# RNN and LSTM in one kernel: from step 48 on, the RNN's input products of 8 steps as seven block products

## The chip, the core and the metric

The kernel runs on one core of a Trainium2 chip. The metric is the device time of one execution in microseconds; smaller is better. Five engines work from queues of their own, each in order: TensorE (PE, with its weight loads as PEld), VectorE (DVE), ScalarE (ACT), GpSimd (POOL), and SyncE (SP), which issues transfers here.

## What is computed

A tanh RNN over 128 steps of x (32 x 128 x 512), its output added to x, then an LSTM over the sum, its output added again. All matrices have 512 rows.

```python
def step(prev_h, xw):                      # RNN, xW = x @ Wx + b
    next_h = jnp.tanh(prev_h @ Wh + xw)
...
x = x + rnn(x, cond_1024, ...)
...
a = xw_t + prev_h @ Wh                     # LSTM, xW = x @ Wx + b, four gates
next_c = f * prev_c + i * g
next_h = o * jnp.tanh(next_c)
...
x = x + lstm(x, cond_1024, ...)
```

## The kernel before

**Steps.** One loop over k runs both networks: iteration k does RNN step k and LSTM step k - LAG, with LAG = 7. x comes in groups of TG = 4 steps (one tile xb, 128 partitions x 512: four slices of 32 batch rows). Every engine has its own copy of the loop, so that the order in each queue is the order in which the functions are called there. "Even" and "odd" below are of k. For k from 27 on the pattern repeats every two steps, apart from work that comes once in a group of 4 steps or rarer.

**Precision.** float32 factors are split into a high and a low float16 half; a product is high x high + high x low (of the weights) + low x high. Each half is scaled by powers of two: the peaks of x over groups of steps are found by `peak_of_x` on VectorE, sent by SyncE through a row on one partition (`peaks_to_row`, `reduce_row`, `peaks_to_all`) and turned into scales (`x_power`, `x_products`, `x_inverses`). Before, one such exchange serves 4 groups (`BATCHES`).

**TensorE in one step.** With 32 batch rows, a matmul has a stationary of 128 x 32 and writes 32 partitions (`quarter(j)`); four of them stand side by side in the array, which is column-tiled. In the order of the queue in step k:
- `recurrent_l(k - 7)`: 48 matmuls with 512 columns, the last 16 with hT_lo;
- for the LSTM's input, pairs of steps are computed by seven block products in place of eight (`block_product`): in an even step 36 matmuls with 256 columns stand here (the rest of block 2, and block 3), in an odd one 60 (the first part of block 2, and blocks 6 and 4);
- `product_r16(k + 1)`: the RNN's input product of the next step, 24 matmuls with 256 columns into the RNN's bank, from x16, the halves of the turned x;
- `recurrent_r16(k)`: 24 matmuls with 256 columns on the RNN's state; the first 16 use hT_r_hi and the last 8 hT_r_lo, for which it waits on `rnn_lo`;
- block 7 in an odd step, blocks 1 and 5 in an even one.

The RNN's outputs come in two halves on other partitions, which `other_half_out` (ScalarE) and `rnn_add_r16` (VectorE) put together.

**ScalarE in one step.** The gates of LSTM step k - 7, a seed or copy for the pairs, tanh of c, once in 4 steps `x16_hi` (k = 4g - 2), in odd steps `y_pair_hi`, xr in two parts, tanh of the RNN, copies and seeds for the pairs, `seed_r(k + 2)` (bias and zeros into the RNN's bank), `rnn_h_hi(k)` (hT_r_hi). Then the next step's gates.

**VectorE in one step.** fc, ig and c of the cell, `rnn_h_lo(k - 1)` (hT_r_lo), h_hi and hT_hi, h_l, h_lo and hT_lo, pre_r, sums for the pairs, once in four steps each `turn_x` (k = 4g - 4), a peak (k = 4g - 19) and `x16_lo` (k = 4g - 2), `y_pair_lo`, the turned hT_r, the scale work.

**GpSimd** adds both outputs to xb and makes the blocks for the pairs. **SyncE** stores group g when it is done, then loads group g + 8 in its place.

## Time and profile before

| | us |
|---|---|
| median of 3 runs | 846.83 |
| lowest, highest | 844.51, 846.87 |
| profiled execution | 844.77 |
| its span in the profile | 843.0 |
| TensorE busy | 827.6 (98%) |
| VectorE busy | 602.5 (71%) |
| ScalarE busy | 578.9 (69%) |
| GpSimd busy | 289.0 (34%) |

A busy TensorE is not one at its peak: matmuls are pipelined and their ends modelled. In an order of time, a line stands for several instructions of one form; the next line's start says more of the pace than the length does. An idle time in brackets names who ended it. Idle time of an engine that nobody waits for costs nothing.

### The profile page before, as it was taken

How to read it: one execution, taken by the hardware profiler on the slowest of the kernel's cores; microseconds unless marked ns; L12 is line 12 of the kernel's file. 1: busy time of each engine (PE TensorE's matmuls, PEld its weight loads, DVE VectorE, ACT ScalarE, POOL GpSimd, SP SyncE). 2: the span in 40 equal slices, each digit the busy share in tenths (PEclk: the TensorE clock that was granted, in tenths of full speed). 3: DMA queues.
4: the chain of work that ended last, by engine and by line, in shares of the span. 5: the costliest groups of instructions: out<-in, count | busy, mean ns of one | idle time of the engine just before them, and what ended most of it. 6: DMA issues, size and time to landing. Idle time of an engine off the chain costs nothing.

```text
span 843.0 us, 52000 instructions
## 1 busy us (share of the span) xinstructions
PE 827.6 (98%) x22859; PEld 620.9 (74%) x22859; DVE 602.5 (71%) x1722; ACT 578.9 (69%) x1542; POOL 289.0 (34%) x642
## 2 busy tenths in 40 slices
...
DMA packets 40195, 30.70 MB, mean 36 GB/s; under 512 B 5772, under 2 KB 38688, under 8 KB 38688
## 3 DMA queue, kind: packets, MB, share of 16 engines
...
q14 instruction: 48, 0.39, 0.2%
q10 hardware_dynamic: 256, 0.11, 0.0%
...
## 4 chain that ended last, share of the span: by engine, by line
PE 90%; DMA 4%; DVE 3%; ACT 2%; issue 1%; SPq 0%; ACTq 0%; DVEq 0%
PE ps_l L1290 34%; PE ps_l L1356 29%; PE ps_r L1442 9%; PE ps_r L1462 8%; PE ps_l L1334 3%; PE ps_l L1303 2%; PE ps_l L1323 2%; DMA wxl_raw<-in_L_cond_Wx 2%; DMA whl_raw<-in_L_cond_Wh 2%; DMA whr_raw<-in_L_cond_Wh 1%; PE ps_r L1413 1%; PE ps_r L1424 1%; DVE ig L1092 0%; PE ps_l L1277 0%; DVE fc L1090 0%
## 5 line engine op out<-in xcount | busy, mean ns | idle before, releaser
L496 POOL TENSOR_TENSOR xb<-xb,h_l 128x128 f32<-128x128 f32 x127 | 58.2, 458 | 383.8 <-DVE h_lo L1125 379.4
L1090 DVE TENSOR_TENSOR fc<-gates,c 128x128 f32<-128x128 f32 x128 | 39.6, 309 | 150.4 <-ACT gates L780 136.5
L1356 PE MATMUL ps_l<-whl_raw,wxl_raw 128*32 128x256 f16 x3816 | 131.6, 273 | 0.0
L1290 PE MATMUL ps_l<-whl_hi,hT_hi 128*32 128x512 f16 x1888 | 122.5, 379 | 1.1 <-DVE hT_hi L1109 1.1
L1290 PE MATMUL ps_l<-whl_hi,hT_lo 128*32 128x512 f16 x1888 | 122.5, 379 | 0.0
L1290 PE MATMUL ps_l<-whl_lo,hT_hi 128*32 128x512 f16 x1888 | 122.4, 379 | 0.0
L1356 PE MATMUL ps_l<-wxl_hi,wxl_raw 128*32 128x256 f16 x2544 | 115.8, 273 | 0.0
L1356 PEld LDWEIGHTS ps_l<-whl_raw,wxl_raw 128*32 128x32 f16 x3816 | 102.1, 97 | 2.2 <-issue 0.2
L780 ACT ACTIVATE gates<-ps_l,g_products 128x256 f32<-128x256 f32 x114 | 53.5, 469 | 54.2 <-PE ps_l L1290 54.1
L1290 PEld LDWEIGHTS ps_l<-whl_lo,hT_hi 128*32 128x32 f16 x1888 | 51.1, 97 | 50.8
L1290 PEld LDWEIGHTS ps_l<-whl_hi,hT_lo 128*32 128x32 f16 x1888 | 51.1, 97 | 50.8
L557 POOL TENSOR_TENSOR whr_raw<-xT,hT_r 128x128 f32<-128x128 f32 x108 | 50.3, 465 | 110.7 <-DVE hT_r L1151 110.7
L532 POOL TENSOR_TENSOR whr_raw<-whr_raw 128x64 f32<-128x64 f32 x216 | 81.2, 396 | 4.2
L1356 PEld LDWEIGHTS ps_l<-wxl_hi,wxl_raw 128*32 128x32 f16 x2544 | 68.4, 97 | 17.6 <-issue 0.2
L803 ACT ACTIVATE h_r<-pre_r 128x128 f32<-128x128 f32 x114 | 35.3, 310 | 65.0 <-DVE pre_r L1136 65.0
L738 ACT ACTIVATE xr<-ps_r,g_products 64x128 f32<-64x128 f32 x114 | 41.5, 364 | 49.1 <-PE ps_r L1442 48.2
L1356 PE MATMUL ps_l<-wxl_lo,wxl_raw 128*32 128x256 f16 x1272 | 71.8, 273 | 0.0
L1290 PEld LDWEIGHTS ps_l<-whl_hi,hT_hi 128*32 128x32 f16 x1888 | 50.7, 97 | 27.3 <-DVE hT_hi L1109 1.3
L1151 DVE STREAM_TRANSPOSE hT_r<-h_r 128x128 f32<-128x128 f32 x128 | 52.6, 411 | 16.7 <-ACT h_r L803 16.6
L762 ACT ACTIVATE hT_r_hi<-hT_r,g_inverses 128x128 f16<-128x128 f32 x114 | 45.5, 399 | 27.7 <-DVE hT_r L1151 23.6
L505 POOL TENSOR_TENSOR xb<-xb,h_r 128x128 f32<-128x128 f32 x128 | 61.7, 482 | 0.0
L1105 DVE SCALAR_TENSOR_TENSOR h_hi<-gates,g_inverses,tanh_c 128x128 f16<-128x128 f32 x122 | 42.9, 352 | 21.7 <-ACT tanh_c L795 15.0
...
## 6 DMA issues: line engine op xcount, KB each, us to landing
xb<-in_x SPq DMA_DIRECT2D x128, 64.0 KB, 2.2
out<-xb SPq DMA_DIRECT2D x124, 64.0 KB, 1.8
...
wxl_raw<-peaks SPq DMA_DIRECT2D x5, 2.0 KB, 2.6
```

The costliest lines, as they stand in the source:

```text
L496: nc.gpsimd.tensor_tensor(xb[g % NX][:, t, :], xb[g % NX][:, t, :], h_l[s % 2][:, :], ALU.add).then_inc(out_done, 1)
L505: nc.gpsimd.tensor_tensor(xb[g % NX][:, t, :], xb[g % NX][:, t, :], h_r[r % 2][:, :], ALU.add).then_inc(y_done, 1)
L532: nc.gpsimd.tensor_tensor(y[:, out, :, :], y[:, a, :, :], y[:, b, :, :], op).then_inc(y_blocks, 1)
L557: nc.gpsimd.tensor_tensor(yA[g % 2][:, first:first + 2, :, t // 2, :], xT[g % 2][:, :, t, :].rearrange("p (a k) b -> p a k b", a=2), hT_r[ ...
L762: nc.scalar.activation(hT_r_hi[:, :, :], hT_r[:, :, :], ACT.Copy, scale=g_scale_r[:, OF_H, g:g + 1]).then_inc(rnn_hi, 1)
L780: nc.scalar.activation(gates[:, 0:2 * P], sums[:, 0:2 * P], ACT.Sigmoid, scale=unscale_l(s)).then_inc(lstm_act, 1)
L1105: nc.vector.scalar_tensor_tensor(out=h_hi[:, :], in0=gates[:, 2 * P:3 * P], scalar=factor, in1=tanh_c[:, :], op0=ALU.mult, op1=ALU.mult).t ...
L1151: nc.vector.transpose(hT_r[:, :, :], by_chunk(h_r[r % 2][:, :])).then_inc(rnn_hT, 1)
L1290: last = nc.tensor.matmul(ps_l[s % 4][quarter(j), :], (hT_hi, hT_lo)[h_part][:, k, :], gate_slice(whl[w_part][k], j), start=False, stop=(h ...
L1356: last = nc.tensor.matmul(at[quarter(j), :], stationary, weights[:, j, :, :], start=False, stop=(y_part == 1 and k == 1), skip_group_check ...
L1442: last = nc.tensor.matmul(ps_r[r % 2][quarter(2 * p + c), 0:2 * P], (hT_r_hi, hT_r_lo)[h_part][:, 2 * p + k, :], quadrant_of_r16(wr[OF_H][ ...
L1462: last = nc.tensor.matmul(ps_r[r % 2][quarter(2 * p + c), 0:2 * P], x16[x_part][g % 2][:, 2 * p + k, t * B:(t + 1) * B], quadrant_of_r16(w ...
```

## The change

From step 48 on, 8 steps (an octet, q = 6 to 15, steps 8q to 8q + 7) have their RNN input products computed as 2 x 2 blocks: the rows are two groups of 4 steps (128 rows each), the inputs and the outputs are halves of 256. Seven block products replace eight (the scheme that the LSTM pairs use already), one in each of the steps 8q - 9 to 8q - 3. All other work of an octet stands ahead of them or behind, by a distance in steps (`ahead(k, ticks)` gives q where k = 8q - ticks):

- 13 and 12: `turn_block` (VectorE) turns the groups 2q and 2q + 1 into a ring of five tiles; 12 and 11: `x_sum` (GpSimd), four sums of 128 x 256.
- 10: `x_rows_high`, `seed_xa` (ScalarE), `x_rows_low` (VectorE). 9: `copy_xm1`, `x_sums_high` part 0, `seed_xd`, `x_sums_low` part 0. 8: `take_xm5`, `x_sums_high` part 1, `x_sums_low` part 1. 7: `copy_xu2`. 6 and 5: `add_xm5`, `add_xu3` (VectorE).
- 4 and 3: `take_x` (ScalarE) copies a bank of 128 x 512 to SBUF; SyncE's `x_inputs` rearranges it by 16 transfers of 32 x 128 into `xin`; `seed_xin` (ScalarE) puts this into the RNN's bank in place of bias and zeros.

Each `x_block` on TensorE is 6 matmuls with a stationary of 128 x 128 and 256 columns, ahead of `recurrent_r16`. The banks ps_pk and ps_end serve for them; a fill opens ps_pk. `product_r16` ends with step 47, `x16_hi` and `x16_lo` with group 11, `turn_x` too. In steps 27 to 33, sums and differences of the RNN's weights are made and split. The peak exchange serves 2 groups from group 12 on, and stands 8 steps earlier.

```diff
-        BATCHES = [(G1, 3)] + [(g, 4) for g in range(4, NG, 4)]
+        BATCHES = [(G1, 3), (4, 4), (8, 4)] + [(g, 2) for g in range(GX, NG, 2)]
...
-        TURN_X_AT.update({4 * g - 4: g for g in range(3, NG)})
+        TURN_X_AT.update({4 * g - 4: g for g in range(3, GX)})
...
-        X16_AT.update({4 * g - 2: g for g in range(RG + 1, NG)})
+        X16_AT.update({4 * g - 2: g for g in range(RG + 1, GX)})
+
+        XW_AT = {27: (0, 1), 28: (2,), 29: (3, 4), 30: (5,), 31: (6, 7)}
+        XW_HALVES_AT = {32: (0, 1), 33: (2, 3)}
+        BIAS_X_AT = 30
+        X_ORDER = (1, 5, 6, 2, 7, 3, 4)
...
+            def x_inputs(q, half):
+
+                sp.wait_ge(x_out, 2 * (q - XQ) + half + 1)
+                sp.wait_ge(xin_zeroed, 1)
+                if q > XQ:
+                    sp.wait_ge(r_seeded, seeds_of_r(8 * (q - 1) + 4 * half + 3))
+                for t in range(TG):
+                    for j in range(J):
+                        sp.dma_start(xin[quarter(j), 4 * half + t, 0, :],
+                                     x_wide[half][quarter(t), j * P:(j + 1) * P]).then_inc(xin_loaded[half], DMA)
...
+                if g % 2 == 0 and XQ <= g // 2 + 1 < NG // 2:
+                    x_inputs(g // 2 + 1, 1)
+                if g % 2 == 1 and XQ <= (g + 3) // 2 < NG // 2:
+                    x_inputs((g + 3) // 2, 0)
...
+            def seed_xin(r):
+                act.wait_ge(rnn_pre, r - 1 - R0)
+                act.wait_ge(xin_loaded[r % 8 // TG], DMA * J * TG * (r // 8 - XQ + 1))
+                nc.scalar.activation(ps_r[r % 2][:, 0:2 * P], xin[:, r % 8, :, :].rearrange("p z u -> p (z u)"),
+                                     ACT.Copy).then_inc(r_seeded, 1)
...
-                if RS <= k + 2 < T:
+                if RS <= k + 2 < 8 * XQ:
                     seed_r(k + 2)
+                if 8 * XQ <= k + 2 < T:
+                    seed_xin(k + 2)
                 if R0 - 1 <= k < T - 1:
                     rnn_h_hi(k)
+                for i in XW_HALVES_AT.get(k, []):
+                    wxr_high(i)
+                if ahead(k, 10) is not None:
+                    x_rows_high(ahead(k, 10))
+                    seed_xa(ahead(k, 10))
+                if ahead(k, 9) is not None:
+                    copy_xm1(ahead(k, 9))
+                    x_sums_high(ahead(k, 9), 0)
+                    seed_xd(ahead(k, 9))
+                if ahead(k, 8) is not None:
+                    take_xm5(ahead(k, 8))
+                    x_sums_high(ahead(k, 8), 1)
+                if ahead(k, 7) is not None:
+                    copy_xu2(ahead(k, 7))
+                if ahead(k, 4) is not None:
+                    take_x(ahead(k, 4), 0)
+                if ahead(k, 3) is not None:
+                    take_x(ahead(k, 3), 1)
...
+                if ahead(k, 13) is not None:
+                    turn_block(2 * ahead(k, 13))
+                if ahead(k, 12) is not None:
+                    turn_block(2 * ahead(k, 12) + 1)
...
+                for x_part, w_part in ((0, 0), (0, 1), (1, 0)):
+                    for k in (0, 1):
+                        first = (w_row + k) * H + w_at
+                        last = nc.tensor.matmul(to, x_home[x_part][:, x_at + k * P:x_at + (k + 1) * P],
+                                                w_home[w_part][:, first:first + HALF], start=False,
+                                                stop=(x_part == 1 and k == 1), skip_group_check=True)
+                last.then_inc(xp_mm, 1)
...
-                elif r < T:
+                elif r < 8 * XQ:
                     product_r16(r)
+                for i, n in enumerate(X_ORDER):
+                    if ahead(r - 1, 9 - i) is not None:
+                        x_block(ahead(r - 1, 9 - i), n)
```

TensorE, an even step before, from the end of the LSTM's recurrent matmuls (L1290, L1356 the LSTM's blocks, L1462 the RNN's input product, L1442 its recurrent matmuls):

```order
L1290 MATMUL ps_l<-whl_hi,hT_lo 32x512 x16
L1356 MATMUL ps_l<-wxl_lo,wxl_raw 32x256 x4
L1356 MATMUL ps_l<-wxl_hi,wxl_raw 32x256 x16
L1356 MATMUL ps_l<-wxl_lo,wxl_raw 32x256 x8
L1356 MATMUL ps_l<-wxl_hi,wxl_raw 32x256 x8
L1462 MATMUL ps_r<-wxr_hi,xT_hi 32x256 x8
L1462 MATMUL ps_r<-wxr_lo,xT_hi 32x256 x8
L1462 MATMUL ps_r<-wxr_hi,xT_lo 32x256 x8
L1442 MATMUL ps_r<-whr_hi,hT_r_hi 32x256 x8
L1442 MATMUL ps_r<-whr_lo,hT_r_hi 32x256 x8
L1442 MATMUL ps_r<-whr_hi,hT_r_lo 32x256 x8
```

The same engine now, step 52 (8q - 4 for q = 7; L1746 is a block with a stationary of 128 x 128, L1641 the LSTM's blocks, L1763 the RNN's recurrent matmuls):

```order
L1575 MATMUL ps_l<-whl_hi,hT_lo 32x512 x16
L1641 MATMUL ps_l<-wxl_lo,wxl_raw 32x256 x4
L1641 MATMUL ps_l<-wxl_hi,wxl_raw 32x256 x16
L1641 MATMUL ps_l<-wxl_lo,wxl_raw 32x256 x8
L1641 MATMUL ps_l<-wxl_hi,wxl_raw 32x256 x8
L1746 MATMUL ps_pk<-wxr_hi,yT 128x256 x2
L1746 MATMUL ps_pk<-wxr_lo,yT 128x256 x2
L1746 MATMUL ps_pk<-wxr_hi,yT 128x256 x2
L1763 MATMUL ps_r<-whr_hi,hT_r_hi 32x256 x8
L1763 MATMUL ps_r<-whr_lo,hT_r_hi 32x256 x8
L1763 MATMUL ps_r<-whr_hi,hT_r_lo 32x256 x8
```

And in step 54 (8q - 2), which has neither:

```order
L1575 MATMUL ps_l<-whl_hi,hT_lo 32x512 x16
L1641 MATMUL ps_l<-wxl_lo,wxl_raw 32x256 x4
L1641 MATMUL ps_l<-wxl_hi,wxl_raw 32x256 x16
L1641 MATMUL ps_l<-wxl_lo,wxl_raw 32x256 x8
L1641 MATMUL ps_l<-wxl_hi,wxl_raw 32x256 x8
L1763 MATMUL ps_r<-whr_hi,hT_r_hi 32x256 x8
L1763 MATMUL ps_r<-whr_lo,hT_r_hi 32x256 x8
L1763 MATMUL ps_r<-whr_hi,hT_r_lo 32x256 x8
```

The 24 column-tiled matmuls of the input product have gone; 6 full-width ones stand in their place, or nothing.

ScalarE, from the tanh of the RNN (L803) in an odd step to the next step's first gates (L780), before:

```order
L803 ACTIVATE h_r<-pre_r 128x128
L671 ACTIVATE ps_l<-bias_l,g_inverses 128x256
L754 ACTIVATE ps_r<-bias_r_and_zeros,g_inverses 128x256
L762 ACTIVATE hT_r_hi<-hT_r,g_inverses 128x128
L780 ACTIVATE gates<-ps_l,g_products 128x256
```

The same now, steps 61 and 62 (8q - 3 and 8q - 2 for q = 8; L910 is `seed_xin`, L964 `take_x`, L989 the gates):

```order
L1012 ACTIVATE h_r<-pre_r 128x128
L821 ACTIVATE ps_l<-bias_l,g_inverses 128x256
L910 ACTIVATE ps_r<-whl_raw 128x256
L971 ACTIVATE hT_r_hi<-hT_r,g_inverses 128x128
L964 ACTIVATE wxl_lo<-ps_end 128x512
L989 ACTIVATE gates<-ps_l,g_products 128x256
```

`take_x` stands between hT_r_hi and the gates.

VectorE, the end of an odd step with scale work (L1024, L1026) and the start of the next (L1090, fc, to L1142, hT_r_lo), before:

```order
L1151 STREAM_TRANSPOSE hT_r<-h_r 128x128
L1083 TENSOR_TENSOR ps_l<-ps_l,wxl_raw 128x256
L1024 TENSOR_SCALAR g_bound<-wxl_raw 128x4
L1026 TENSOR_SCALAR g_power<-g_bound 128x4
L1090 TENSOR_TENSOR fc<-gates,c 128x128
L1092 TENSOR_TENSOR ig<-gates 128x128
L1094 TENSOR_TENSOR c<-fc,ig 128x128
L1142 SCALAR_TENSOR_TENSOR hT_r_lo<-hT_r,g_inverses,hT_r_hi 128x128
```

Now, at the end of a step 8q - 5 and the start of 8q - 4 (L1152 is `turn_block`, L1183 `add_xu3`, L1411 hT_r_lo):

```order
L1420 STREAM_TRANSPOSE hT_r<-h_r 128x128
L1352 TENSOR_TENSOR ps_l<-ps_l,wxl_raw 128x256
L1152 STREAM_TRANSPOSE wxl_raw<-xb 128x4x4x32
L1183 TENSOR_TENSOR ps_end<-ps_end,wxl_raw 128x256
L1293 TENSOR_SCALAR g_bound<-peak_wide 128x2
L1295 TENSOR_SCALAR g_power<-g_bound 128x2
L1359 TENSOR_TENSOR fc<-gates,c 128x128
L1361 TENSOR_TENSOR ig<-gates 128x128
L1363 TENSOR_TENSOR c<-fc,ig 128x128
L1411 SCALAR_TENSOR_TENSOR hT_r_lo<-hT_r,g_inverses,hT_r_hi 128x128
```

A turn and a sum have come ahead of the scale work; the turn stood in the middle of an even step before.

## Rows read from the trace of the kernel before

**Rows 1.** The page, busy time: engine, busy us (share of the span), instructions
```profile
PE 827.6 (98%) x22859; PEld 620.9 (74%) x22859; DVE 602.5 (71%) x1722; ACT 578.9 (69%) x1542; POOL 289.0 (34%) x642
```
**Rows 2.** Table by stretch: busy us of PE, PEld, DVE, ACT, POOL; then clock, DMA
```profile
400.00:500.00 100.00, 100.00 (x2924) 77.93 (x2916) 73.45 (x221) 70.34 (x200) 33.05 (x80) 1.00 0.10 25
```
**Rows 3.** Order of time, TensorE, an even step: start us, length us, group
```profile
423.54 0.28 PE L1356 MATMUL ps_l<-wxl_lo,wxl_raw 128*32 128x256 f16 x4
...
424.53 0.39 PE L1462 MATMUL ps_r<-wxr_hi,xT_hi 128*32 128x256 f16 x8
...
424.96 0.39 PE L1462 MATMUL ps_r<-wxr_hi,xT_lo 128*32 128x256 f16 x8
425.18 0.39 PE L1442 MATMUL ps_r<-whr_hi,hT_r_hi 128*32 128x256 f16 x8
...
425.62 0.39 PE L1442 MATMUL ps_r<-whr_hi,hT_r_lo 128*32 128x256 f16 x8
```
**Rows 4.** Order of time, weight loads, the same step
```profile
425.52 0.21 PEld L1442 LDWEIGHTS ps_r<-whr_hi,hT_r_lo 128*32 128x32 f16 x8
```
**Rows 5.** Order of time, VectorE, the same step
```profile
425.12 0.34 DVE L1142 SCALAR_TENSOR_TENSOR hT_r_lo<-hT_r,g_inverses,hT_r_hi 128x128 f16<-128x128 f32 x1
```
**Rows 6.** Order of time, TensorE, the last RNN step
```profile
803.17 0.39 PE L1442 MATMUL ps_r<-whr_lo,hT_r_hi 128*32 128x256 f16 x8
803.53 0.40 PE L1442 MATMUL ps_r<-whr_hi,hT_r_lo 128*32 128x256 f16 x8
```
**Rows 7.** Order of time, VectorE, the last RNN step
```profile
803.13 0.34 DVE L1142 SCALAR_TENSOR_TENSOR hT_r_lo<-hT_r,g_inverses,hT_r_hi 128x128 f16<-128x128 f32 x1
```
**Rows 8.** Order of time, TensorE, around the fill behind the RNN
```profile
808.25 0.83 PE L1356 MATMUL ps_l<-wxr_raw,wxl_raw 128*32 128x256 f16 x24
809.01 0.39 PE L1490 MATMUL ps_r<-ident 128*128 128x512 f16 x1
809.33 0.40 PE L1356 MATMUL ps_l<-wxl_hi,wxl_raw 128*32 128x256 f16 x8
```
**Rows 9.** Order of time, TensorE, the start of the program
```profile
6.29 1.47 PE L1490 MATMUL ps_l<-ident 128*128 128x512 f16 x6
8.16 1.08 PE L1413 MATMUL ps_r<-wxr_raw,xT 128*32 128x128 f32 x32 [0.40 <-DMA wxr_raw<-in_L_cond_Wx]
9.17 0.60 PE L1490 MATMUL ps_pk<-ident 128*128 128x512 f16 x2
```
**Rows 10.** Order of time, weight loads, the fill of rows 8
```profile
809.01 0.10 PEld L1490 LDWEIGHTS ps_r<-ident 128*128 128x128 f16 x1 [0.21 <-issue]
```
**Rows 11.** Order of time, ScalarE, first gates of four steps, idle time ahead
```profile
429.96 0.47 ACT L780 ACTIVATE gates<-ps_l,g_products 128x256 f32<-128x256 f32 x1 [0.88 <-PE ps_l L1290]
...
436.15 0.47 ACT L780 ACTIVATE gates<-ps_l,g_products 128x256 f32<-128x256 f32 x1 [0.43 <-PE ps_l L1290]
...
442.35 0.47 ACT L780 ACTIVATE gates<-ps_l,g_products 128x256 f32<-128x256 f32 x1 [0.72 <-PE ps_l L1290]
...
448.60 0.46 ACT L780 ACTIVATE gates<-ps_l,g_products 128x256 f32<-128x256 f32 x1
```
**Rows 12.** Groups by form, ScalarE: busy us, mean ns of one, idle before
```profile
L622 ACT ACTIVATE xT_hi<-xT,g_inverses 128x512 f16<-128x512 f32 x29 | 20.5, 707 | 0.0
L671 ACT ACTIVATE ps_l<-bias_l,g_inverses 128x256 f32<-128x256 f32 x53 | 24.5, 462 | 0.0
```
**Rows 13.** Order of time, VectorE, an odd step with scale work and the next
```profile
287.26 0.38 DVE L1026 TENSOR_SCALAR g_power<-g_bound 128x4 int32<-128x4 int32 x1
288.04 0.29 DVE L1090 TENSOR_TENSOR fc<-gates,c 128x128 f32<-128x128 f32 x1 [0.40 <-ACT gates L780]
```
**Rows 14.** Groups by form, VectorE, the turn of x
```profile
L913 DVE STREAM_TRANSPOSE xT<-xb 128x512 f32<-128x512 f32 x32 | 36.5, 1142 | 3.7 <-DMA xb<-in_x 3.7
```
**Rows 15.** Instructions of one line, the loads: issue on SyncE, ns min/median/max; landing us
```profile
L420 SPq DMA_DIRECT2D xb<-in_x x128: 322/432/1822, 0.7 to 655.6; - x128
...
DMA to landing us min/median/max: 1.8/2.2/6.6
```

More of the change, by code:

```diff
@@ L39 @@
 RS = R0 + 2
+XQ = 6
+GX = 2 * XQ
 def rnn_lstm_kernel(nc, x, h0, WxR, WhR, bR, WxL, WhL, bL, out):
```

252 lines of the change are left out of this document (240 added, 12 removed).

## The prediction

> **What bounds the kernel now.** I read the busy shares first, then the table by stretch, then the orders of time of TensorE, VectorE and ScalarE in one pair of steps. TensorE is busy for 827.6 of 843.0 us [rows 1], and from 200 to 800 us it is never idle (six rows like the one shown, 100.00 of 100.00), at full clock, while VectorE stands at 73 and ScalarE at 70 [rows 2]. So a matmul removed from these steps is time gained, if nothing that TensorE waits for comes too late. A step takes 6.19 us. Let T0 be the moment at which the LSTM's recurrent matmuls end (423.54 in the even step of [rows 3]). Then come 36 block matmuls of the LSTM, the 24 RNN input matmuls (424.53 to 425.18, 0.65 us), and the 24 recurrent matmuls of the RNN, whose last 8 use hT_r_lo.
>
> The share of 100% hides how near the next limit is. The weight load of those last 8 starts at 425.52 [rows 4]; VectorE has hT_r_lo at 425.12 + 0.34 = 425.46 [rows 5]. The slack is **0.06 us**. hT_r_lo stands in VectorE's queue behind the LSTM cell of the same step, and the cell behind ScalarE's gates. So in an even step, if the RNN's recurrent matmuls come earlier or the gates later, TensorE stops. In an odd step 60 matmuls stand ahead instead of 36 and the slack is about 0.8 us. The trace has one step that already has no input product, the last one: its hT_r_lo (803.13 + 0.34 = 803.47 [rows 7]) comes too late, and the matmuls that should follow 0.22 us behind their neighbours at 803.17 start at 803.53 [rows 6], 0.14 us late, although there the recurrent matmuls run in halves, so that the gates start before the last of them end.
>
> **Part 1: the matmuls.** 80 products (steps 48 to 127) of 24 column-tiled matmuls go: 80 x 0.656 = 52.5 us. 70 blocks (7 for each of 10 octets) come, each of 6 matmuls with a 128x128 stationary and 256 columns. The tiled matmuls pass 256 columns in 0.109 us (8 of them, two rounds, in 0.219 [rows 3]); the full-width fills pass 512 columns in (1.47 - 0.39)/5 = 0.216 us each with a weight load for each [rows 9], and such a load takes 0.10 us [rows 10], under 0.109. So the loads are hidden and six take 0.656 us: 45.9 us. Were loads not hidden, 70 x 6 x 0.1 = 41 us would come on top; the pace of the fills speaks against it. The saving is 6.6 us so far; the fill that opens the new bank gives back 0.4.
>
> But each block is a full-width excursion among column-tiled matmuls. The trace has one in the dense part, the fill at 809.01. The 24 tiled matmuls before it start at 808.25, and their successor would start at 808.25 + 0.656 = 808.91. The fill starts at 809.01, lasts 0.216 at pace, and the next tiled matmul starts not at 809.23 but at 809.33 [rows 8]; the view puts the idle time down to issue, not to a semaphore [rows 10]. Early in the program it is the same: 32 tiled matmuls (eight rounds of 0.1125) from 8.16 would end at 9.06, and the fill starts at 9.17 [rows 9]. An excursion costs **0.10 us on each side, 0.21 in all**; 70 of them are 14.7 us. The bounds are 0 (the pipeline carries over) and 0.21; I take 0.21, a row of exactly this pair of shapes. Part 1: 52.5 - 45.9 - 0.4 - 14.7 = 8.5 us slower.
> The Trainium skill, page TensorEngine Tiling (Array Packing), section Key Properties, says that changing the tiling mode drains TensorE. It gives no price; by that rule, too, every block pays twice, and the trace agrees with 0.10 us for each switch.
>
> **Part 2: the steps left without a product.** Seven of eight steps hold a block where the product stood; step 8q-2 holds neither (54, 62, ... 110), nor do steps 118 to 126. In an even one of these, hT_r_lo would be needed 0.66 us sooner and has 0.06 of slack: 0.60 of the 0.66 is not gained. That is 13 steps (8, and 118, 120, 122, 124, 126): **+7.8 us**. The four odd ones of the tail gain in full, since they have the slack.
>
> **Part 3: the work that lands ahead of the gates.** ScalarE's new instructions stand at the end of a step, behind hT_r_hi and ahead of the next gates. Start to start, 512 columns cost 0.65 us (0.71 less the overlap), a seed of 256 0.40 [rows 12], a PSUM copy of 256 0.30. ScalarE's idle time ahead of the next gates was 0.88 or 0.72 at the end of an even step, 0.43 at that of an odd one, and none where the odd step has a peak reduction, whose gates start 0.06 late (448.60, 6.25 after 442.35) [rows 11]. VectorE is ready 0.40 us ahead of fc where it has g_bound and g_power at the end of an odd step [rows 13]. With a block the slack of an even step is 0.06 + 0.21 = 0.27. Then, per octet:
> - step 8q-10: rows high (0.65 + 0.30) and a seed (0.40), 1.35 against some 0.8: gates of 8q-9 0.55 late; odd, it costs nothing.
> - step 8q-9 (odd): 0.30 + 0.65 + 0.40 = 1.35 against 0.43: 0.92 late in even step 8q-8, less 0.27: **0.65**.
> - step 8q-8 (even): 0.95 against 0.7 and the pause just had: nothing. Step 8q-7 (odd, peaks): a copy, 0.30 + 0.06, less 0.27: 0.09.
> - step 8q-5 (odd): VectorE gets a turn (1.14 [rows 14], 1.06 start to start), the last sum (0.35) and the power of two that already stands in rows 13: 1.41 - 0.40 = 1.0 late, less 0.27: **0.73** in 8q-4.
> - step 8q-4: take_x (512 columns) against 0.7: nothing. Step 8q-3 (odd, peaks): take_x, 0.60 + 0.06 = **0.66** late in step 8q-2, which has neither block nor slack.
>
> Over the octets: 10 x 0.66 + 9 x 0.65 + 8 x 0.73 + 9 x 0.09 = 19.1 (the first octet's blocks stand beside the old product, with 0.66 us more of slack). Once only, the weight blocks of step 33 (two halves, 1.3 us behind a peak step) and the first turn and power in step 35: 1.3 + 0.6 = 1.9. Part 3: **+21.0 us**, the least sure part. Its lower bound is 0, if the tails overlap better than start-to-start times say; its upper bound is about 30, if no late start is caught up in the odd steps.
>
> Costed at nothing: the recurrent matmuls now wait for a seed that ScalarE issues two steps ahead; GpSimd's four sums of 128x256 per octet (GpSimd is busy for 33 of 100 us [rows 2]) wait in its queue behind add_yT and add_y, whose readers come a step later; x16_hi and x16_lo vanish from steps that did not need the room; the finer peak exchange is read a step after it is made. SyncE gets 32 transfers per octet. The first 16 start when take_x of step 8q-4 ends; ScalarE waits for them at the seed in step 8q-2, some 11.9 us later. An issue takes 0.43 us, the first after a pause up to 1.8, and landing 2.2 [rows 15]: 1.8 + 15 x 0.43 + 2.2 = 10.5. They fit with 1.4 to spare; the other 16 have four steps.
>
> **Sum.** 8.5 + 7.8 + 21.0 = 37.3 us. Against the profiled execution of 844.8 (span 843.0 and 1.8 around it) that is 882.1; the median, 846.8, is 2 above it, which I leave out: **882**.
>
> **The rivals.**
> - *TensorE alone decides* (0.13): the tails of ScalarE and VectorE are absorbed and hT_r_lo comes in time. Then only part 1 counts: 844.8 + 8.5 = 853. Against it stand the 0.06 us of slack and the late start in [rows 6].
> - *The seeds arrive late* (0.14): SyncE's 16 transfers take 0.75 us each instead of 0.43 (what a burst of four costs on average, 3.1 us by these numbers), 12 + 2.2 = 14.2 against 11.9. ScalarE stops 2.3 us per octet with hT_r_hi and the gates behind it; less the slack of an odd step some 1.8 reach TensorE, x 10: 900.
> - *Faster* (0.06): the switch costs nothing where the queue of matmuls is full, and the block's own time covers the tails. The place is the 70 block boundaries; the price is nothing and 6.6 - 0.4 = 6.2 us are gained: 838.6. It decides below 0.09 us per excursion (6.2/70); the one excursion in the trace shows 0.21, and parts 2 and 3 would have to vanish as well.
> - *No change* (0.03): the gains of seven for eight and the switches happen to cancel at about 0.09 us per excursion: 845.
>
> **How the numbers follow.** The forecast has 0.60, with its own range 864 to 892 from part 3; 0.04 is left for something above 900. From 850 to 900 the range holds the forecast, the first rival and about half of the second, 0.8. Within 0.3% (about what a measurement of this kernel can tell from no change) I put 0.03; faster 0.06; slower 0.91.
>
> **What would show it.** In the profile after: gaps of 0.10 on both sides of each group of six full-width matmuls, which itself lasts 0.66; TensorE idle in even steps ahead of the recurrent matmuls with hT_r_lo, released by VectorE; steps of 6.4 us with a block, 6.1 to 6.8 at 8q-2; ScalarE's gates late behind take_x and the high halves. The forecast is wrong low or high if full-width matmuls start without a gap, if steps 8q-8, 8q-4 and 8q-2 show no pause, or if the seed waits for a DMA.

## The result: 891.5 us, 5.5% slower

The changed kernel takes 891.45 us (median of 6 executions, 890.01 to 893.66) against 844.75 of the kernel before beside it: a ratio of 1.0552, interval 1.0536 to 1.0569. The forecast was 882 with a range of 850 to 900. The direction and the main mechanism were right; 9 us are missing from the sum, and inside it several terms were off and partly cancelled. Of the runs below, two executions of e6_tiled and one of the kernel before were disturbed and are left out, so that e6_tiled's ratio rests on two executions.

The busy times of the profiled execution after, as in [rows 1]:

```profile
span 888.2 us, 49723 instructions
...
PE 847.0 (95%) x21360; PEld 599.0 (67%) x21360; DVE 636.8 (72%) x1791; ACT 607.4 (68%) x1636; POOL 314.7 (35%) x692
```

The span grew by 45.2 us, TensorE's busy time by 19.4 only. Where [rows 2] had 100.00 of 100.00 us busy, the same view by stretches now shows idle time on TensorE, still at full clock (columns: us, then PE, PEld, DVE, ACT, POOL busy, granted clock, DMA share, GB/s):

```profile
420.00:520.00 100.00, 94.53 (x2410) 67.05 (x2406) 72.27 (x215) 70.60 (x203) 33.69 (x84) 1.00 0.14 34
```

The table of waits says who released TensorE (us in total, times, longest), and below it one row of ScalarE's:

```profile
PE ps_r L1763 <- DVE hT_r_lo L1411: 19.2, 20, 1.6
PE ps_pk L1746 <- DVE wxl_hi L1165: 6.6, 7, 1.6
PE ps_end L1746 <- DVE yT L1171: 4.3, 9, 0.5
...
ACT ps_r L910 <- DMA whl_raw<-wxl_lo: 9.5, 8, 1.9
```

hT_r_lo was forecast as the late one, and it is. The two rows at L1746 are blocks that wait for their operand (x_lows and x_sums_low, which share names with other rings), and the row of ScalarE is a seed that waits for a transfer, 8 times: that was a rival.

**Where the 45 us are.** I took the length of each step as the distance between the starts of the LSTM's recurrent matmuls (first row with whl_hi and hT_hi) of one step and the next. Before, it is 6.19 for every step from 28 to 125. The differences after, summed by kind of step, beside what the terms of the prediction give for the same steps:

| steps | how many | forecast, us | measured, us | a step takes |
|---|---|---|---|---|
| 28 to 37, the weight block is made | 10 | 2.3 | 6.6 | up to 7.93 |
| 38 to 46, first octet beside the old product | 9 | 6.7 | 7.9 | 7.05 to 7.12 |
| 8q-7, 8q-6, 8q-5, 8q-3 (block and nothing else late) | 36 | 8.4 | 7.9 | 6.41 |
| 8q-8 (block, after the tail of 8q-9) | 9 | 7.7 | 6.9 | 6.98 |
| 8q-4 (block, after the turn) | 9 | 7.7 | 2.6 | 6.49, the last 6.41 |
| 8q-2 (neither) | 8 | 4.8 | 6.8 | 7.11, the last 6.52 |
| 8q-9 (block, seed of the step after next) | 9 | 1.9 | 9.1 | 6.41 to 8.10 |
| 118 to 125, tail | 8 | -2.2 | -2.3 | even 6.05, odd 5.54, but 6.38 in 119 |
| sum | | 37.3 | 45.4 | |

The sum came closer than its terms: the rows forecast too low miss 14.7 us together, and those forecast too high give 6.6 of it back, most of it at 8q-4. So the small distance from 882 to 891 is in part luck.

Five rows carry the story: the 6.41 (part 1), the tail (part 2), 8q-4, 8q-2 with the first row, and 8q-9.

### The profile page after: what moved, and what is told of

Same layout as the page of the kernel before. It is cut to its first block, busy times and chain, and to the rows that moved or that the text cites. A ratio compares the mean times of both kernels' runs of the same rounds, so it can differ in the third digit from the quotient of the medians.

```text
span 888.2 us, 49723 instructions
## 1 busy us (share of the span) xinstructions
PE 847.0 (95%) x21360; PEld 599.0 (67%) x21360; DVE 636.8 (72%) x1791; ACT 607.4 (68%) x1636; POOL 314.7 (35%) x692
## 4 chain that ended last, share of the span: by engine, by line
PE 58%; DVE 13%; ACT 10%; SPq 9%; issue 6%; DMA 2%; ACTq 0%; DVEq 0%
PE ps_l L1575 21%; PE ps_l L1641 15%; SPq L546 9%; PE ps_r L1763 6%; PE ps_l L1619 3%; DMA whl_raw<-wxl_lo 2%; PE ps_pk L1746 2%; PE ps_end L1746 2%; PE ps_l L1588 2%; DVE fc L1359 2%; PE ps_r L1783 1%; PE ps_l L1608 1%; DVE ig L1361 1%; DVE c L1363 1%; ACT gates L989 1%
## 5 line engine op out<-in xcount | busy, mean ns | idle before, releaser
L1641 PE MATMUL ps_l<-whl_raw,wxl_raw 128*32 128x256 f16 x3816 | 131.6, 273 | 0.0
L1641 PE MATMUL ps_l<-wxl_hi,wxl_raw 128*32 128x256 f16 x2544 | 116.0, 273 | 0.0
L1359 DVE TENSOR_TENSOR fc<-gates,c 128x128 f32<-128x128 f32 x128 | 48.0, 375 | 92.1 <-ACT gates L989 77.7
L1641 PEld LDWEIGHTS ps_l<-whl_raw,wxl_raw 128*32 128x32 f16 x3816 | 102.1, 97 | 2.2 <-issue 0.2
L1641 PEld LDWEIGHTS ps_l<-wxl_hi,wxl_raw 128*32 128x32 f16 x2544 | 68.7, 97 | 17.5 <-issue 0.2
L989 ACT ACTIVATE gates<-ps_l,g_products 128x256 f32<-128x256 f32 x114 | 53.0, 465 | 31.0 <-PE ps_l L1575 30.0
L1641 PE MATMUL ps_l<-wxl_lo,wxl_raw 128*32 128x256 f16 x1272 | 72.0, 273 | 0.0
L626 POOL TENSOR_TENSOR whr_raw<-whr_raw 128x64 f32<-128x64 f32 x216 | 67.8, 335 | 4.2
L1004 ACT ACTIVATE tanh_c<-c 128x128 f32<-128x128 f32 x128 | 39.2, 306 | 39.1 <-DVE c L1363 36.4
L971 ACT ACTIVATE hT_r_hi<-hT_r,g_inverses 128x128 f16<-128x128 f32 x114 | 45.2, 396 | 28.8 <-DVE hT_r L1420 24.4
L1763 PE MATMUL ps_r<-whr_hi,hT_r_lo 128*32 128x256 f16 x912 | 45.1, 274 | 19.3 <-DVE hT_r_lo L1411 19.2
L599 POOL TENSOR_TENSOR xb<-xb,h_r 128x128 f32<-128x128 f32 x128 | 59.5, 465 | 0.0
```

Source lines behind the costliest of these rows:

```text
L599: nc.gpsimd.tensor_tensor(xb[g % NX][:, t, :], xb[g % NX][:, t, :], h_r[r % 2][:, :], ALU.add).then_inc(y_done, 1)
L626: nc.gpsimd.tensor_tensor(y[:, out, :, :], y[:, a, :, :], y[:, b, :, :], op).then_inc(y_blocks, 1)
L971: nc.scalar.activation(hT_r_hi[:, :, :], hT_r[:, :, :], ACT.Copy, scale=g_scale_r[:, OF_H, g:g + 1]).then_inc(rnn_hi, 1)
L989: nc.scalar.activation(gates[:, 0:2 * P], sums[:, 0:2 * P], ACT.Sigmoid, scale=unscale_l(s)).then_inc(lstm_act, 1)
L1359: nc.vector.tensor_tensor(fc[:, :], gates[:, P:2 * P], c[:, :], ALU.mult).then_inc(lstm_fc, 1)
L1641: last = nc.tensor.matmul(at[quarter(j), :], stationary, weights[:, j, :, :], start=False, stop=(y_part == 1 and k == 1), skip_group_check ...
```

## Part 1 on the chip: a block costs its switch, and e1_tiled takes the switch away

TensorE after, step 39, where the old product and a block stand side by side (start, us, tile, count):

```profile
265.75 0.39 PE L1783 MATMUL ps_r<-wxr_hi,xT_lo 128*32 128x256 f16 x8
266.07 0.39 PE L1746 MATMUL ps_pk<-wxr_hi,wxl_hi 128*128 128x256 f16 x2
266.30 0.38 PE L1746 MATMUL ps_pk<-wxr_lo,wxl_hi 128*128 128x256 f16 x2
266.52 0.38 PE L1746 MATMUL ps_pk<-wxr_hi,wxl_hi 128*128 128x256 f16 x2
266.83 0.40 PE L1763 MATMUL ps_r<-whr_hi,hT_r_hi 128*32 128x256 f16 x8
```

Eight tiled matmuls pass in 0.22, so the block could start at 265.97: it starts at 266.07. Two full-width ones also pass in 0.22 (266.07, 266.30, 266.52), so the next tiled could start at 266.74: it starts at 266.83. No semaphore is named as the end of either pause. That is 0.10 and 0.09, as [rows 8] had it.

**e1_tiled** runs the same block as column tiles, same operands and bank:

```diff
-                        last = nc.tensor.matmul(to, x_home[x_part][:, x_at + k * P:x_at + (k + 1) * P],
-                                                w_home[w_part][:, first:first + HALF], ...)
+                        for j in range(J):
+                            at = x_at + k * P + j * B
+                            last = nc.tensor.matmul(to[quarter(j), :], x_home[x_part][:, at:at + B],
+                                                    w_home[w_part][:, first:first + HALF], ...)
```

> The changed kernel (891.5 us), with each of a block's 6 full-width matmuls (stationary 128x128) issued as four column-tiled ones of 128x32, so that the array never leaves its column-tiled mode; all else is as in the changed kernel. Theory (each change between full width and column tiles drains TensorE, 0.11 us a side): the undisturbed block steps fall from 6.41 to 6.19 us, and the gaps of 0.10 around the blocks vanish. Where a pause for hT_r_lo or for a block's operand stands in the step, part of the 0.22 goes into the pause. 70 blocks x 0.22 = 15.4, of which about 50 count in full: 880 us (878 to 884). Rival (the 0.22 is the price of a block's waits on semaphores, or of its weight loads, not of the mode): the steps stay at 6.41 and the time at 891.

Measured: 886.49 us, ratio 1.048 (1.0449 to 1.0512). TensorE in step 57:

```profile
389.33 0.83 PE L1641 MATMUL ps_l<-wxr_raw,wxl_raw 128*32 128x256 f16 x24
389.98 0.83 PE L1748 MATMUL ps_pk<-wxl_raw,yT 128*32 128x256 f16 x24
390.64 0.39 PE L1765 MATMUL ps_r<-whr_hi,hT_r_hi 128*32 128x256 f16 x8
```

The block lasts 0.66 as before, but both gaps are gone, and each odd step with a block falls from 6.41 to 6.19. So the 0.22 goes with the change between full width and column tiles, not with the six matmuls' own time, nor with the block's semaphores, which the edit keeps. One thing the two runs don't separate. The first weight load behind the change starts together with its matmul:

```profile
266.07 0.11 PEld L1746 LDWEIGHTS ps_pk<-wxr_hi,wxl_hi 128*128 128x128 f16 x2 [0.21 <-issue]
```

The loads inside the block start 0.11 ahead of theirs (266.30 for the matmul at 266.41) and are hidden. A load lasts 0.10, as long as the gap. So the price may be the change itself, or one weight load in each direction that can't be hidden behind matmuls of the other form.

The total fell by 5.0 and not by the 11 us expected. Steps with a pause (8q-8, 8q-4) hold their length, since their pause only grows into the room, and in this profile the transfers of 8q-9 came later still (13.6 us in place of 9.1). This profiled execution also took 889.9 us, 3.4 above the run's median: step 28 starts 3.2 later than in the changed kernel's profile (188.7 against 185.5), of which TensorE waits 2.5 for a load of the LSTM's weights, which has nothing to do with the edit. e6_tiled below is the same edit without these disturbances.

The Trainium skill, page TensorEngine Tiling (Array Packing), section Key Properties, says that changing the tiling mode drains TensorE, and gives no price. The two runs agree that a change costs something, 0.10 us each; whether it is a drain they don't show.

## The late seeds: e3_sems

The issue queue of SyncE after, around step 54 (start, us, count):

```profile
359.07 11.72 SPq L546 DMA_DIRECT2D whl_raw<-wxl_lo  x16
377.04 12.53 SPq L546 DMA_DIRECT2D whl_raw<-wxl_lo  x16
```

and the seed of step 56 on ScalarE, at the end of step 54:

```profile
373.28 0.39 ACT L910 ACTIVATE ps_r<-whl_raw 128x256 f32<-128x256 f32 x1 [1.79 <-DMA whl_raw<-wxl_lo]
```

Sixteen issues take 11.72 us, 0.73 each: the rival's 0.75, not the forecast's 0.43, which was the issue of another kind (64 KB loads from memory, [rows 15]). The last lands 1.8 us later by the median landing of this line, about 372.6, and the seed starts at 373.28. hT_r_hi and the high parts of the next block stand behind it on ScalarE, so the block of step 55 is 1.62 us late:

```profile
376.23 0.39 PE L1746 MATMUL ps_pk<-wxr_hi,wxl_hi 128*128 128x256 f16 x2 [1.62 <-DVE wxl_hi L1165]
```

The seed of one step needs 4 transfers, but its semaphore counted all 16. **e3_sems** gives each step's four a semaphore of their own:

```diff
-        xin_loaded = [sem("first_rnn_inputs_in_place"), sem("last_rnn_inputs_in_place")]
+        xin_loaded = [sem(f"rnn_inputs_{i}_in_place") for i in range(8)]
...
-                act.wait_ge(xin_loaded[r % 8 // TG], DMA * J * TG * (r // 8 - XQ + 1))
+                act.wait_ge(xin_loaded[r % 8], DMA * J * (r // 8 - XQ + 1))
```

> The changed kernel with a semaphore for each step's 4 transfers in place of one for 16, so that the seed of step 8q (issued in step 8q-2) waits for the first 4 transfers of its half and not for all. Theory (SyncE's issues, 0.59 us each, are too slow for 16 in the time between take_x and the seed): ScalarE's waits for these transfers (9.5 us in all, up to 1.9) vanish, and steps 8q-9, 0.2 to 1.9 us above the kernel before (9.1 in sum over nine), come down to 6.4 to 6.6: 884 us (883 to 887). Rival (step 8q-9 is long because the first block waits for the low halves of x behind ScalarE's tail, whatever the transfers do): 8q-9 keeps at least half of its excess, 888 or more.

Measured: 882.06 us, 1.0437 (1.0414 to 1.0461). The class 8q-9 goes from 9.1 to 2.0 us, every step of it 6.41, ScalarE's row with the DMA is gone from the waits, and the other classes stay within 0.8: 8q-8 gives 0.8 more and the tail, where step 119 had a late seed too, 0.7, so that the steps fall by 8.6 in all. The total came 0.9 below the range expected. The transfers are as slow as before (median issue 0.59 us in both); only what waits for them changed. The rival was right as a mechanism and cost 7.1 us in these steps instead of its 18, since every octet was late by less than the 1.8 it assumed: steps 8q-9 of the nine octets took 6.41, 8.10, 7.35, 7.28, 6.77, 7.68, 6.74, 6.41 and 8.07.

## Step 8q-2 and the weight block: GpSimd holds VectorE

The prediction put 8q-2 down to take_x ahead of the gates and costed GpSimd's additions at nothing. VectorE, TensorE and GpSimd after, step 54:

```profile
366.95 0.47 DVE L1359 TENSOR_TENSOR fc<-gates,c 128x128 f32<-128x128 f32 x1 [0.88 <-ACT gates L989]
367.35 0.28 DVE L1361 TENSOR_TENSOR ig<-gates 128x128 f32<-128x128 f32 x1
367.66 0.70 DVE L1363 TENSOR_TENSOR c<-fc,ig 128x128 f32<-128x128 f32 x1
368.28 0.34 DVE L1411 SCALAR_TENSOR_TENSOR hT_r_lo<-hT_r,g_inverses,hT_r_hi 128x128 f16<-128x128 f32 x1
...
368.67 0.40 PE L1763 MATMUL ps_r<-whr_hi,hT_r_lo 128*32 128x256 f16 x8 [1.39 <-DVE hT_r_lo L1411]
...
366.54 0.73 POOL L712 TENSOR_TENSOR wxl_raw<-wxl_raw,xT 128x256 f32<-128x256 f32 x1
367.35 0.85 POOL L712 TENSOR_TENSOR wxl_raw<-xT,wxl_raw 128x256 f32<-128x256 f32 x1
```

Before, the three operations of the cell take 0.29 each; here fc ends 0.15 behind the first GpSimd sum (367.42 after 367.27) and c as far behind the second (368.36 after 368.20). ig, which starts just ahead of the second sum, passes at its usual 0.28, and it is the sum that takes 0.85 in place of 0.73. TensorE then waits 1.39 us for hT_r_lo. In step 28, where GpSimd makes the weight block, the rows of VectorE and GpSimd show it larger:

```profile
188.79 0.84 DVE L1359 TENSOR_TENSOR fc<-gates,c 128x128 f32<-128x128 f32 x1
189.54 1.24 DVE L1361 TENSOR_TENSOR ig<-gates 128x128 f32<-128x128 f32 x1
190.82 0.29 DVE L1363 TENSOR_TENSOR c<-fc,ig 128x128 f32<-128x128 f32 x1
...
188.32 2.31 POOL L676 TENSOR_TENSOR whl_raw<-wxr_hi,wxr_lo 128x512 f32<-128x512 f16 x2
```

Two GpSimd operations of 1.15 each end at 189.48 and 190.63; fc ends at 189.63 and ig at 190.78, 0.15 behind each. Three runs test this against the take_x theory.

**e7_probe** is the kernel *before* with one GpSimd addition of 128x256 at the end of odd steps from 49 on, and nothing else:

```diff
+                if 48 <= k < 118 and k % 2:
+                    rows = wxl_raw[1]
+                    nc.gpsimd.tensor_tensor(rows[:, 4 * HALF:5 * HALF], rows[:, 2 * HALF:3 * HALF], rows[:, 3 * HALF:4 * HALF], ALU.add)
```

> The kernel before (844.8 us) with one more addition of 128x256 on GpSimd at the end of each odd step from 49 to 117 (of tiles that nobody needs; the result goes nowhere). Theory (VectorE's additions and products of two SBUF operands wait while GpSimd does a wide one, and an even step has 0.1 us of slack): GpSimd's addition of 0.7 us runs from 0.1 us after T0 to 0.9, where VectorE does fc and ig; these are held by 0.3 to 0.5 us, and the 34 even steps behind take 6.4 to 6.7 us in place of 6.19: 855 us (852 to 861). Rival (the two engines do not touch each other, and the long c and ig of the changed kernel have another cause): 844.8, fc and ig at 0.29.

Measured: 851.45 us, 1.0072 (1.0047 to 1.0097), the span 6.6 longer, of which 5.8 lies in 15 even steps, 8q-6 and 8q-2 where a peak reduction stands ahead: 6.58 in place of 6.19. The other steps from 48 on stay, so the total is 0.6 below the range, which had all 34 even steps grow. A peak reduction makes hT_r and so GpSimd's queue later, and only then does the addition run beside fc and ig for longer than the slack; the one step 8q-2 of the changed kernel without it, 110, takes 6.52 in place of 7.11. VectorE and GpSimd in one that grows (step 54, ig) and in one that doesn't (step 56, fc):

```profile
351.29 0.29 DVE L1093 TENSOR_TENSOR fc<-gates,c 128x128 f32<-128x128 f32 x1 [0.51 <-ACT gates L783]
351.55 0.77 DVE L1095 TENSOR_TENSOR ig<-gates 128x128 f32<-128x128 f32 x1
...
351.38 0.80 POOL L594 TENSOR_TENSOR wxl_raw<-wxl_raw 128x256 f32<-128x256 f32 x1
```

```profile
364.02 0.41 DVE L1093 TENSOR_TENSOR fc<-gates,c 128x128 f32<-128x128 f32 x1 [1.05 <-ACT gates L783]
364.36 0.28 DVE L1095 TENSOR_TENSOR ig<-gates 128x128 f32<-128x128 f32 x1
...
363.56 0.72 POOL L594 TENSOR_TENSOR wxl_raw<-wxl_raw 128x256 f32<-128x256 f32 x1
```

An addition that nobody waits for lengthens a step by 0.39 us, if it runs late enough beside the cell. The Trainium skill, page SBUF — State Buffer, section Who interferes with whom, says that a VectorE instruction with two SBUF inputs contends with a GpSimd instruction that reads SBUF; these rows agree (0.29 becomes 0.77, and the end falls 0.15 behind GpSimd's), and by that rule the sums should have had a price in the prediction.

**e4_take** is e3_sems with the second take_x moved ahead of rnn_h_hi, so that the gates of 8q-2 no longer stand behind it:

```diff
+                if ahead(k, 3) is not None:
+                    take_x(ahead(k, 3), 1)
                 if R0 - 1 <= k < T - 1:
                     rnn_h_hi(k)
...
-                if ahead(k, 3) is not None:
-                    take_x(ahead(k, 3), 1)
```

> The kernel with a semaphore for each 4 transfers (882.1 us) and take_x of the second half ahead of rnn_h_hi in step 8q-3, where ScalarE used to wait some 0.8 us for hT_r, instead of behind it, ahead of the gates. Theory (in step 8q-2 GpSimd's two sums at the end of 8q-3 hold VectorE's ig and c until they are done, whenever the gates come; step 38 shows 7.05 us without any take_x): 8q-2 stays at 6.9 to 7.1, 881 us (880 to 882.5). Rival (the prediction's: take_x makes the gates 0.66 late, and this alone is the pause): 8q-2 falls from 7.11 to about 6.5, 877 us.

Measured: 880.82 us, 1.0413 (1.0389 to 1.0437), as GpSimd's theory had it; 8q-2 takes 7.05 in place of 7.11, where the rival had 6.5. The gates come earlier, and the cell gives it back:

```profile
366.25 0.29 DVE L1360 TENSOR_TENSOR fc<-gates,c 128x128 f32<-128x128 f32 x1 [0.39 <-ACT gates L990]
366.51 0.77 DVE L1362 TENSOR_TENSOR ig<-gates 128x128 f32<-128x128 f32 x1
367.31 0.77 DVE L1364 TENSOR_TENSOR c<-fc,ig 128x128 f32<-128x128 f32 x1
```

**e2_gpsimd** leaves take_x and moves GpSimd's additions instead, to the middle of odd steps, where the cell isn't running:

```diff
-        XW_AT = {27: (0, 1), 28: (2,), 29: (3, 4), 30: (5,), 31: (6, 7)}
+        XW_AT = {27: (0, 1), 29: (2, 3), 31: (4, 5), 33: (6, 7)}
...
+                if ahead(k, 11) is not None:
+                    x_sum(ahead(k, 11), 1)
+                    x_sum(ahead(k, 11), 3)
...
                 if k < T:
                     add_yT(k)
```

> The changed kernel with GpSimd's wide additions moved: the sums of the x blocks stand ahead of add_yT in steps 8q-11 and 8q-9 (before: at the end of 8q-12 and 8q-11), and the pieces of the RNN weight blocks ahead of add_yT in steps 27, 29, 31, 33 (before: at the end of 27 to 31), with their high and low halves in 34 and 35. So they run while GpSimd used to wait for hT_r, and not while VectorE computes fc, ig and c. Theory (VectorE's additions and products of two SBUF operands wait for GpSimd's wide ones; in the changed kernel c took 0.70 and ig up to 1.24 us in place of 0.29 where GpSimd ran beside them): ig and c stand at 0.29 in steps 8q-2, those steps fall from 7.11 by some 0.4 us, and the steps 28 to 37 from 6.6 us above the kernel before to about 2: 883 us (881 to 886). Rival (the pauses come from ScalarE's tails alone): 8q-2 stays at 7.1 and the time within 1.5 us of 891.

Measured: 892.42 us, 1.0558 (1.0534 to 1.0582), so the total missed its expectation by 9. The steps aimed at did what was expected: 8q-2 falls from 7.11 to 6.58, steps 28 to 37 from 6.6 us to 2.8 (1.5 of it in step 36, where the edit puts two subtractions on the weight halves, 1.29 us together, behind VectorE's turn and ahead of fc). With 1.2 in the first octet that is a gain of 8.8 us. 5.3 of it went back in 8q-9, which cost 14.4 in place of 9.1 (the late transfers again), and 2.7 in 8q-8, 9.5 in place of 6.9, for which no cause was looked for. Another 3.8 us lie ahead of step 28 (189.3 against 185.5): TensorE waits 2.3 there for a load of the LSTM's weights, before any of the edit runs.

Together: neither cause alone makes 8q-2. Without GpSimd's share 0.53 is gone (e2_gpsimd), without take_x's 0.06 (e4_take), and without both (e8_slots) the step takes 6.12, against 6.05 in the tail where neither exists. So take_x costs 0.46 (forecast 0.66), but only once GpSimd no longer covers it, and GpSimd 0.93 once take_x is gone. Both figures lean on e8_slots, which moves other work as well.

## Part 2: e5_noprod and e11_noprod

**e5_noprod** is the kernel before without the RNN's input product from step 48 on, and nothing in its place:

```diff
-                elif r < T:
+                elif r < 48:
                     product_r16(r)
```

> The kernel before, with the RNN's input product left out from step 48 on and nothing put in its place (the RNN runs on without x there; seeds, halves of x and all else stay). 80 products x 0.656 us = 52.5 us of TensorE's work. Theory (in even steps hT_r_lo, behind ScalarE's gates and VectorE's cell, is the next limit with some 0.1 us of slack; in odd steps the slack is 0.8): odd steps fall from 6.19 to 5.54 us, even ones only to about 6.05: 40 x 0.656 + 40 x 0.14 = 31.8, 813 us (810 to 818). Rival (TensorE alone decides): all steps fall to 5.54, 792 us.

Measured: 817.39 us, 0.9671 (0.9648 to 0.9694). Odd steps fall by 0.65 to 5.54; even ones take 6.05, or 6.28 behind a peak step, longer than the 6.19 with the product. TensorE and VectorE in step 54:

```profile
348.68 0.39 PE L1444 MATMUL ps_r<-whr_lo,hT_r_hi 128*32 128x256 f16 x8
349.63 0.40 PE L1444 MATMUL ps_r<-whr_hi,hT_r_lo 128*32 128x256 f16 x8 [0.56 <-DVE hT_r_lo L1142]
...
349.23 0.34 DVE L1142 SCALAR_TENSOR_TENSOR hT_r_lo<-hT_r,g_inverses,hT_r_hi 128x128 f16<-128x128 f32 x1
```

So about half of the 52.5 us that leave TensorE is not gained (28 are), and TensorE's wait in even steps is for hT_r_lo. **e11_noprod** is e5_noprod with the LSTM's first pair block (24 matmuls of 0.65 us) put ahead of the RNN's recurrent matmuls in even steps:

```diff
+                m1_first = k < T and pair_at(k) is not None and k > 46
+                if m1_first:
+                    pair_m1(pair_at(k))
                 if R0 <= k < T:
                     recurrent_r16(k)
```

> The kernel before without the RNN's input product from step 48 on (it left out 80 products and came to 817.4 us, even steps 6.05 and 6.28, odd ones 5.54), with block 1 of the LSTM pair ahead of the RNN's recurrent matmuls in even steps. Theory (the even steps' loss is the position of the hT_r_lo matmuls, not work): even steps fall to 5.54 to 5.65, 797 us (794 to 802), and most of the 52.5 us of TensorE's work shows. Rival (the chain of the LSTM is as near as that of the RNN): 6.0 stays, 815 or more.

Measured: 797.30 us, 0.9427 (0.9410 to 0.9443). The same work on TensorE as e5_noprod in another order, 20 us less. Steps take 5.54 to 5.63, but for four of 6.16 (59, 75, 91, 107), where VectorE reduces the row of the peaks (1.06 us) ahead of pre_r. Of hT_r_lo's 16.4 us of waits (39 times) 1.0 is left (4 times, in these steps). That shows part 2: in all other steps no engine is short of time, only the place of eight matmuls was too early.

## What the mended change is worth: e6_tiled, e8_slots, e9_first, e10_first

**e6_tiled** is e4_take with the column-tiled block of e1_tiled.

> The kernel of the run before in this set (a semaphore for each 4 transfers, take_x early), with the blocks column-tiled too. Theory (each change of mode costs 0.11 us a side; in even steps that already pause, the block's 0.22 was hidden in part): odd block steps 6.19, steps 8q-6 6.39, the paused ones as they are: some 9 us less than without the tiling, 872 us (870 to 874). Rival (the pauses take up what the switches gave): less than 4 us are gained, 877 or more.

Measured: 871.01 and 870.98 us, 1.0299 (1.0263 to 1.0335). Odd steps take 6.19, 8q-6 6.39. It is 9.8 us less than e4_take, of the 14.7 that part 1 has for the switches; the rest went into the steps with a pause, as in e1_tiled.

**e8_slots** adds the other remedies: GpSimd's additions in the middle of odd steps, one weight half in each of steps 34 to 37, the memset in step 41, and ScalarE's work on x spread over its idle time:

```diff
                 if ahead(k, 10) is not None:
-                    x_rows_high(ahead(k, 10))
+                    x_row_22_high(ahead(k, 10))
                     seed_xa(ahead(k, 10))
                 if ahead(k, 9) is not None:
-                    copy_xm1(ahead(k, 9))
                     x_sums_high(ahead(k, 9), 0)
-                    seed_xd(ahead(k, 9))
```

(what is removed here stands ahead of the RNN's tanh in the same or the next step).

> All remedies at once: column-tiled blocks, a semaphore for each 4 transfers, take_x early, GpSimd's sums and weight pieces ahead of add_yT in odd steps, the zeros in step 41, the weight halves one per step in 34 to 37, and ScalarE's copies and seeds for the blocks spread over its idle times ahead of the RNN's tanh (the first high half in 8q-10, seed_xd in 8q-9, copy_xm1 in 8q-8, take_xm5 in 8q-7) and ahead of rnn_h_hi (copy_xu2 in 8q-7). Theory (the pauses are those three causes and nothing else): setup steps at most 2 us above the kernel before, first octet 4.6, octets within 0.3 us of the kernel before each, the tail 2.9 below: 850 us (847 to 853). It can't be much below the kernel before, since the step without a block is an even one and gains 0.1 of its 0.66. Rival (VectorE's and ScalarE's added work of 4 us per octet finds no room at all): 860 or more.

Measured: 854.09 us, 1.0107 (1.0074 to 1.0140), 1.1 above the range. By the steps only 8.7 us of the 45.4 are left: 1.9 in steps 28 to 37, 5.4 in 38 to 46 (the doubled steps), 2.6 in 8q-8 and 2.6 in 8q-4, less 3.2 in the tail and 0.6 in 8q-2; the other steps with a block take 6.19, as with the product.

**e9_first** and **e10_first** put the LSTM's first pair block ahead of the recurrent matmuls, as in e11_noprod: e9_first in steps 8q-2 and from 119 on, e10_first also in 8q-8 and 8q-4. The difference between the two:

```diff
-                m1_first = k < T and pair_at(k) is not None and (k > 118 or 47 < k and k % 8 == 6)
+                m1_first = k < T and pair_at(k) is not None and (k > 47 and k % 8 != 2 or k > 118)
```

> The kernel with all remedies (854.1 us); in the even steps that have neither product nor block (54, 62, ... 118, and 120 to 126) TensorE does the LSTM pair's block 1 (24 matmuls, 0.66 us) ahead of the RNN's recurrent matmuls instead of behind them. Theory (these steps lose most of the 0.66 us to the wait for hT_r_lo, and the block fills it): 8q-2 falls from 6.12 to 5.6, the even ones of the tail from 6.05 to 5.54: 8 x 0.5 + 5 x 0.5 = 6.5, 847.5 us (846.5 to 850). Rival (the LSTM's own chain, recurrent matmuls to hT_hi, is next at once in even steps): less than 2 us gained, 852 or more.

> As the run before in this set, and the same order in the even steps 8q-8 and 8q-4 as well, where 0.28 and 0.31 us are still lost to a late hT_r_lo. Theory (any late hT_r_lo is covered by work that can stand ahead of it, and ScalarE has 0.7 us of idle time at the end of an even step for the RNN's chain, which now ends 0.66 later): both come down to 6.2 to 6.25, 9 x 0.28 + 8 x 0.31 = 5.0 less: 843 us (841.5 to 846). Rival (the later hT_r_hi pushes the next gates, and the odd steps grow): no gain against the run before, or a loss.

Measured: e9_first 851.43 us, 1.0068 (1.0052 to 1.0083); 8q-2 takes 5.54 (5.0 us under the steps of before), the tail 5.2 under, but 8q-8 rises from 6.47 to 6.89 and gives 3.3 back. e10_first 848.19 us, 1.0026 (1.0012 to 1.0039): 8q-4 falls to 6.19, 8q-8 stays at 6.91. Both missed by 4 to 5 us, by the same step. TensorE in step 56 of e10_first:

```profile
370.20 0.39 PE L1650 MATMUL ps_l<-wxl_hi,wxl_raw 128*32 128x256 f16 x8
371.12 0.84 PE L1757 MATMUL ps_end<-wxl_raw,yT 128*32 128x256 f16 x24 [0.53 <-DVE yT L1180]
371.79 0.39 PE L1650 MATMUL ps_l<-wxl_hi,wxl_raw 128*32 128x256 f16 x8
```

The block itself waits for its operand, x_sums_low, and it stands ahead of the moved pair block, so the move can't help it. This is not a matter of hT_r_lo, as I had taken it in both expectations. In the changed kernel, too, 0.50 of the pause of 8q-8 stands ahead of the block:

```profile
382.56 0.83 PE L1746 MATMUL ps_end<-wxl_raw,yT 128*128 128x256 f16 x6 [0.50 <-DVE yT L1171]
```

What shows why it is later in e9_first than in e8_slots is only a difference in order of time: hT_r is ready 0.43 us later against the recurrent matmuls (369.43 and 370.06, against 368.00 and 369.06), and the sums' high half stands behind it on ScalarE. Most of the 0.43 is one operation ahead of hT_r on VectorE: y_pair_lo (L1211) takes 0.94 us in steps 56, 64 and 72 of e9_first (from 368.56, while a GpSimd sum runs from 368.29 to 369.02), and 0.67 in e8_slots, where it starts as that sum ends. That resembles the hold of e7_probe, but it is another operation and ends 0.48 behind the sum; no run tested it.

## The prediction, step by step

- **What bounds the kernel: right.** TensorE with 0.06 us of slack behind it on hT_r_lo. The longest row of waits after is that one, 19.2 us.
- **Part 1: right to a few per cent.** A block costs 6.41 - 6.19 = 0.22 more than the product; 0.21 was forecast from one row of [rows 8], and e1_tiled and e6_tiled show that it goes with the change of form. Both rivals that let the switch be free are out, and so is *TensorE alone decides*: e5_noprod came to 817 us where that would have had 792.
- **Part 2: right.** Even steps of the tail take 6.05, so 0.14 is gained in place of 0.06; odd ones 5.54, 0.65. e5_noprod and e11_noprod show the mechanism.
- **Part 3: a total of 21.0 that hides errors both ways.** 8q-8: 0.65 forecast, 0.57 measured beside the switch, but most of it is the block's operand and not hT_r_lo. 8q-4: 0.73 forecast, 0.08 measured. The turn and the sum come where forecast (406.70 to 408.06, 1.36), but the step that failed is "1.41 - 0.40 = 1.0 late". It kept the two scale operations at the 0.75 us they took before (286.89 to 287.64, [rows 13]), and here, in the rows of step 60 below, they take 0.27 (408.06 to 408.33). That leaves fc 0.48 late against its step's start in place of 1.0; less the slack of 0.27 it is 0.2, of which 0.08 shows. 8q-2: 0.66 forecast for take_x, 0.46 without GpSimd's share, and 0.53 more with it. The weight block: 1.9 forecast, 6.6 measured, of which e8_slots, with the same work at other places, keeps 1.9. That 1.9 was also forecast is chance: the forecast had it for ScalarE's two halves and the turn, and gave GpSimd nothing.
- **"Costed at nothing: GpSimd's four sums": wrong.** I looked at what waits in GpSimd's queue, not at what its operations do to VectorE. With the weight pieces this is 3.8 us in steps 28 to 37 and 3.8 in 8q-2 (e2_gpsimd, which moves the weight halves by two steps as well).
- **"They fit with 1.4 to spare": wrong.** The 0.43 us per issue was that of another transfer. Here sixteen take 10.7 to 12.8 us, and 7.1 us of the steps 8q-9 (8.6 of all steps, 9.4 of the medians) come from it (e3_sems), about as much as the distance from 882 to 891. The rival for this had its own slip: 2.3 us per octet less the slack of 0.8 that the prediction gives an odd step is 1.5, not 1.8.

VectorE in step 60, for 8q-4:

```profile
407.75 0.41 DVE L1183 TENSOR_TENSOR ps_end<-ps_end,wxl_raw 128x256 f32<-128x256 f32 x1
408.06 0.16 DVE L1293 TENSOR_SCALAR g_bound<-peak_wide 128x2 f32<-128x2 f32 x1
408.25 0.17 DVE L1295 TENSOR_SCALAR g_power<-g_bound 128x2 int32<-128x2 int32 x1
408.33 0.29 DVE L1359 TENSOR_TENSOR fc<-gates,c 128x128 f32<-128x128 f32 x1
```

**What stays open.** Whether the 0.10 us of a change is a drain or a weight load; the rest of why hT_r is later in 8q-8 of e9_first; the 0.3 that 8q-4 and 8q-8 keep in e8_slots. Step 38, which takes 6.91 in e8_slots though no block stands there, waits 0.53 for hT_r_lo: by the trace the last weight half (0.62 us on ScalarE ahead of the gates, 0.69 on VectorE up to 253.35) holds fc back to 253.41. The best version found, e10_first, is at 1.0026 of the kernel before. What seven blocks for eight bring there does not pay for the doubled steps of the first octet (5.4 us), the waits of 8q-8 (6.0) and the weight block (1.9).
